# A third buffer for gathered rows, half the DMA descriptor scratch, and gathers paced eight tiles lower

## The reference

```python
final_scores, pk_idx = jax.lax.top_k(score, FINAL_TOPK)
final_indices = jnp.take_along_axis(index, pk_idx, axis=-1)
final_scores = jax.nn.softmax(final_scores, axis=-1)
...
k = jnp.einsum('bnhk,bnhkd->bnhd', kv_scores, keys_table[ind])
v = jnp.einsum('bnhk,bnhkd->bnhd', kv_scores, values_table[ind])
```

## Time and profile before

| | |
|---|---|
| time, three runs | 3266.03, 3269.42, 3277.52 us; median 3269.42 |
| profiled execution | no time of its own is given beside its span |
| its span, first to last instruction | 3918.28 us |
| span over median time | 1.198 |
| mean granted TensorE clock | 0.862 |
| longest busy engine | PE, 3008.9 us |

### The profile page before, as it was taken

One profiled execution on the slowest core, in us unless ns is written; L12 is line 12 of the kernel. 1 busy time (PEld: TensorE's weight loads), 2 busy tenths in 40 slices (PEclk: granted clock), 3 DMA queues, 4 the chain that ended last, 5 costly groups with the idle time before them and its releaser, 6 DMA issues.

```text
span 3918.3 us, 39268 instructions
## 1 busy us (share of the span) xinstructions
PE 3008.9 (77%) x9722; PEld 1391.1 (36%) x9722; DVE 2785.8 (71%) x9999; ACT 2039.4 (52%) x4498; POOL 2057.7 (53%) x2095
## 2 busy tenths in 40 slices
PE   4861657878787878878778868888778878888888
PEld 2430223333333333333333433333333433333343
DVE  7678777777777777776777887777768786874433
ACT  3231545555555555655555655556555655555532
POOL 3011666666656665555565655556656655655400
PEclk8985777888787888989888989888888988989899
DMA  1001121212121111112121212111111212121100
GB/s 37 22 8 52 44 66 43 62 45 57 48 56 47 52 52 50 52 46 55 44 59 38 65 40 57 44 52 53 51 50 46 57 46 56 42 62 39 33 3 3
DMA packets 85626, 179.86 MB, mean 46 GB/s; under 512 B 40177, under 2 KB 41107, under 8 KB 85398
## 3 DMA queue, kind: packets, MB, share of 16 engines
q0 software_dynamic: 66560, 135.40, 13.1%
q1 hardware_dynamic: 18838, 41.94, 3.5%
HBM read 176.15 MB, written 1.05 MB: 45 GB/s over the span
## 4 chain that ended last, share of the span: by engine, by line
PE 41%; DVE 25%; another core or an unknown queue 11%; issue 8%; ACT 8%; ACTq 0%; DVEq 0%
PE mx_acc L1430 12%; PE mx_O L1442 7%; PE mx_area L1476 6%; DVE mx_W L1787 5%; PE mx_D L1420 4%; ACT mx_GT L1691 3%; DVE mx_KVs L2013 3%; PE mx_area L1456 2%; ACT mx_W L1623 2%; DVE mx_mx_part L2031 2%; PE mx_area L1492 1%; DVE mx_mx L2031 1%; PE mx_X L1560 1%; PE mx_area L1486 1%
## 5 line engine op out<-in xcount | busy, mean ns | idle before, releaser
L1402 POOL DMA_INDIRECT mx_G<-in_kv_table,mx_slot_i x2048 | 2004.0, 978 | 1394.6 <-issue 590.1
L1430 PE MATMUL mx_acc<-mx_W,mx_table 128*128 128x512 f32 x2048 | 1180.7, 660 | 1.6 <-ACT mx_kvT L1630 0.7
L1787 DVE SCALAR_TENSOR_TENSOR mx_W<-mx_D,mx_W 128x512 f32<-128x512 f32 x1024 | 699.1, 683 | 297.5 <-ACT mx_W L1623 180.5
L1623 ACT ACTIVATE mx_W<-mx_D 128x512 f32<-128x512 f32 x1024 | 606.6, 593 | 523.2 <-PE mx_D L1420 231.0
L1691 ACT ACTIVATE mx_GT<-mx_G,mx_slot_w 128x128 f32<-128x128 f32 x2048 | 759.2, 495 | 3.2 <-DVE mx_KVs L2013 1.1
L1420 PE MATMUL mx_D<-mx_U,mx_pick_b 96*128 96x512 bf16 x1024 | 432.7, 423 | 110.8 <-DVE mx_W L1787 52.5
L1430 PEld LDWEIGHTS mx_acc<-mx_W,mx_table 128*128 128x128 f32 x2048 | 436.1, 214 | 201.9 <-issue 104.5
L1647 ACT ACTIVATE mx_PT<-mx_area 128x512 f32<-128x512 f32 x472 | 241.8, 514 | 464.9 <-PE mx_area L1480 146.3
L1442 PE MATMUL mx_O<-mx_PT,mx_KVs 128*65 128x512 f32 (+3 forms) x768 | 347.5, 536 | 170.0 <-ACT mx_PT L1647 82.8
L1456 PE MATMUL mx_area<-mx_KTa,mx_QTa 64*128 64x512 f32 (+3 forms) x384 | 200.6, 607 | 132.6 <-DVE mx_mx L2031 66.1
L2013 DVE TENSOR_REDUCE mx_KVs<-mx_GT 128x128 f32<-128x2048 f32 x128 | 291.9, 2280 | 6.0 <-ACT mx_GT L1691 5.9
(11 more groups left out here) (390 smaller groups left out, 4462.4 us busy)
## 6 DMA issues: line engine op xcount, KB each, us to landing
mx_table<-in_kv_dense SPq DMA_DIRECT2D x64, 512.0 KB
mx_G<-in_kv_table,mx_slot_i POOLq DMA_INDIRECT x2048
tz_table<-in_c_dft SPq DMA_DIRECT2D x1, 2048.0 KB
tz_table<-in_c_idft SPq DMA_DIRECT2D x8, 256.0 KB, 2.6
out_h<-mx_xc SPq DMA_DIRECT2D x4, 256.0 KB
mx_G<-in_c_pick SPq DMA_DIRECT2D x1, 528.0 KB
st_h<-in_tok_W,em_ids POOLq DMA_INDIRECT x32
st_keys<-in_pk_keys SPq DMA_DIRECT2D x1, 512.0 KB, 3.9
```

The source lines that it names most:

```text
L1402: pool.indirect_dma_start(G[g % RING][:, r, :], None, a["kv_table"], bass.IndirectOffsetOnAxis(slot_i[n % 2][:, k, r:r + 1], 0))\
L1430: pe.matmul(acc[:, :], table[:, tile, :], W[c % TILE_RING][:, :], start=(tile == 0), stop=(tile == TILES - 1)).then_inc(applied, 1)
L1623: act.activation(W[c % TILE_RING][:, :], D_ps[c % 3][:, :], ACT.Exp).then_inc(p_done, 1)
L1787: dve.scalar_tensor_tensor(W[c % TILE_RING][:, :], D_ps[c % 3][:, :], 0.0, W[c % TILE_RING][:, :], ALU.is_ge, ALU.mult).then_inc(w_done, 1)
```

## The change

`RING` goes from 2 to 3, so that three groups of rows can be in SBUF. The wait `scaled` of group `g` asks for the scaling of `g - 3` in place of `g - 2`. The tile number in the `w_done` wait is eight lower: gather `r` of block `k` now waits for mask `64 n + 8 k - 14 + r // 2`. The descriptor scratch is set to 8192 bytes, which gives the third buffer its 8192 bytes.

```diff
-RING = 2
+RING = 3
...
                 if g >= RING:
                     pool.wait_ge(scaled, g - RING + 1)
                 for r in range(TOPK):
-                    ahead = SLOT * n + 8 * k - 6 + r // 2
+                    ahead = SLOT * n + 8 * k - 14 + r // 2
                     if r % 2 == 0 and ahead > 0:
                         pool.wait_ge(w_done, ahead)
                     pool.indirect_dma_start(G[g % RING][:, r, :], None, a["kv_table"],
...
-    nc = bacc.Bacc("TRN2", target_bir_lowering=False, num_devices=1)
+    nc = bacc.Bacc("TRN2", target_bir_lowering=False, num_devices=1, dynamic_dma_scratch_size=8192)
```

## The result

| kernel | median | runs | lowest to highest |
|---|---|---|---|
| before | 3271.77 us | 4 | 3266.03 to 3277.52 us |
| changed | 3231.67 us | 4 | 3230.03 to 3232.88 us |

The ratio is 0.9872, with a 95% interval of 0.9851 to 0.9893: 1.3% faster, some 40 us. The forecast was 3265 us with a range of 3238 to 3290, so the time lies outside, on the fast side. The nearest to it was the rival "POOL is nearly the bound", with 3237 us.

What follows compares the result with a forecast made beforehand. The prediction took the mixer's round trip PE, ACT, DVE, PE of dense tiles and attention as the bound. Its terms, -4 us for buffer and pacing and 0 for the rest, took 3269.4 to 3265 us, range 3238 to 3290.

Steps and rivals of the forecast that it cites:

- POOL is nearly the bound: Rival, faster: at 94% POOL load unevenness makes ACT wait; half the pairs gain 32 us, so 3237 us; chance 0.30.
- Step 1: Third buffer and pacing eight tiles lower: removes ACT's wait for rows, -4 us, bounds 0 and 64 us.
- Step 4: Half the descriptor scratch: 18 more ring turns, 7 to 35 us of POOL, hidden by idle time; cost taken 0.
- step 2: POOL's own time: 2048 gathers of 1.27 us unchanged, its idle time not on the path and merely moving; 0 us.
- Step 3: First pair: the first group's last two gathers go at once, but ACT takes the group no sooner; 0 us.
- Step 5: SBUF: the buffer takes exactly what the scratch gives up, and the bytes moved are the same; 0 us.
- DMA vanishes from the releasers: Sign in the profile after: ACT's idle time before scaling falls from 3.2 to about 1 us, none ended by DMA.
- the wait for masks: Sign in the profile after: POOL's idle time before gathers for masks stays near 547 us.
- The lead of 35 us: Sign near 1960 us: a group's last gather is issued some 35 us before ACT's use, in place of 10.3.
- then the traced run misleads about POOL's share: Failure sign: time falls by over 10 us while the profile's ACT idle time was 1.1 us already.
- Nothing changes: Rival: gathers shrink with the rest, ACT never waits, earlier rows lie in their buffer; 3269 us; chance 0.22.
- Ring turns on the path: Rival, slower: 18 more ring turns each delay ACT by up to 1.95 us; 3304 us, half of them 3287; chance 0.13.

Runs made afterwards that it cites:

- second profile of before: The kernel before, unchanged, profiled once more because its first profile had a span of 3918 us; measured 3265.75 us, span 3263.9 us.

## Why the prediction was wrong

*The bound.* "POOL waits for the others, and hardly anybody waits for POOL" was read off rows of an execution 20% too long. I saw the factor, worked out both loads, 94% if gathers keep their length and 76% if not, and then let the row of the disturbed trace decide ("one row in 128 shows a wait"). The gathers did keep their length: 2600 us in 2720 before, 2595 in 2668 after. The working was right, the choice was not. This is the step that failed first, and it carried the two terms below down with it.

*Step 1, buffer and pacing: the mis-sized term.* The direction and the mechanism hold (uneven stretches turn into waits of ACT, and it takes buffer and pacing together to remove them). Forecast -4 us, measured about -22 on top of the scratch. My own estimate of a tight place (4.0 us late) was fair, since waits of ACT of 4.4 us stand in the second profile of before. Its number was wrong: not one group but 60 of 128 made ACT wait there, and 32 in the changed kernel. Carried down to "one in 128" by the wrong trace, the term was off by a factor of five. (The period of 26.3 us is a small slip: the rows divided by 127 run from the first gather to the last, 15 gathers too far; the trace has 26.2.)

*Step 4, the scratch: wrong in sign.* I saw the pauses and their period, and took a period of 112 for one turn of the ring, so half the ring for twice as many. The runs show no pause at half, three quarters and seven eighths of the size. The price was put at 0 to 35 us with no gain; it gave 20. I had tied "hidden by POOL's idle time" to idle time that the timed runs don't have; had the pauses been priced as they stand, their loss would have been up to 29 us of gain on a loaded POOL. The rule that a ring too small for what is made "would lengthen the gather itself" found nothing to bear it out: down to 4096 bytes gathers stayed at 0.975 to 0.984 us, and with 2048 at 0.970, the pause standing in front of the gather.

*Steps 2, 3 and 5.* In step 2 the number and the length of the gathers hold. That POOL's idle time "is not on the path and merely moves" does not: without the disturbance it was 87.0 + 33.0 us in place of 681, and POOL is on the path. Step 3 put the first group at 0; ACT starts it at 371.7 in place of 373.2 us, without a wait in both. Step 5 holds as far as the sizes of the scratch tell, since they move the buffers and don't change the time.

*What was to be seen in the profile.* "DMA vanishes from the releasers" was false, and the wait for masks was 56.1 us and not near 547. The lead of 35 us was false too: group 62 is issued last at 1630.78 and read at 1636.17, 5.4 us later. The sentence on what would make the prediction fail ("then the traced run misleads about POOL's share") names what happened.

*The rivals.* "POOL is nearly the bound" had the mechanism, but its 3237 us came near by luck: 32 us for buffer and pacing, where some 22 were measured, and none of the 20 us that came from the scratch. "Nothing changes" fell with its premise, that the gathers shrink. "Ring turns on the path" was right that such pauses lie on the path and wrong on which size has them.

## What to carry to other kernels

When the profile's span and the timed runs disagree by more than a few us, take no wait from it. Here lengths of operations carried over to 1% on POOL, ACT and DVE, and not on PE, whose line 1430 took 660 ns in place of 620. Add up for each engine what it must do, its issue time included, against the timed run; here that gave 94%, and 96% was measured. The scratch of DMA descriptors is a setting worth trying by itself, since pauses at a fixed count of gathers, with nothing to release them, are a cost that can go.

## What the runs showed of the hardware

An indirect DMA of 128 rows of 512 bytes took POOL 0.94 us and 0.30 us of issue as the median in every run, 1.25 us from one to the next, and landed 2.5 us after its start (the last of a group in the second profile of before, as the median). In the changed kernel 274 of the 2048 were longer than 1.0 us, up to 1.95. They fall together with certain operations of DVE: none of the 55 gathers that meet no operation of DVE is among them, and none of the 212 that meet the `match_replace` of line 1808, but 30 of the 32 that meet the `tensor_tensor` of line 1938, whose two inputs are both in SBUF. The number of such inputs alone doesn't sort them: of the 31 that meet the `tensor_tensor` of line 1844, also with two, only 2 are stretched, and of the 47 that meet the `tensor_scalar` of line 1940, with one, 30 are. The Trainium skill says in "SBUF — State Buffer", section "Who interferes with whom", that a DVE operation with two SBUF inputs and a GpSimd operation that reads SBUF shut each other out; by that rule a gather, if it reads its row numbers there, would be stretched. The same section says that in a probe `tensor_tensor` did not hold up a DMA issued by GpSimd. The trace agrees with the rule in part (line 1938) and not throughout (line 1844), and no run took such an operation away, so the cause stays open.

The default scratch of 16384 bytes had pauses of about 2 us at each 112th gather, 2048 bytes 2.2 to 2.3 us at each 16th (a group has 16 gathers too, so the count may be the group's), and 4096, 8192, 12288 and 14336 none. 4096 was tried with three and four buffers only.
